# Gram-Schmidt beside an attention kernel: vectors kept as rows, the step's row spread by DMA

## What is computed

```python
def gram_schmidt(X):            # X: 256 x 32
    r = X.shape[1]
    Q = X
    for i in range(r):
        q = Q[:, i]
        q = q / (jnp.linalg.norm(q) + EPS)
        Q = Q.at[:, i].set(q)
        coeffs = q @ Q[:, i + 1:]
        Q = Q.at[:, i + 1:].add(-jnp.outer(q, coeffs))
    return Q
U_o = gram_schmidt(U)
V_o = gram_schmidt(V)
basis = U_o @ V_o.T
```

## Time and profile before

| | |
|---|---|
| runs | 1352.56, 1354.65, 1354.92 us |
| the profiled execution | 1352.78 us, of which 1350.6 us are the span of the trace |
| busy, share of the span | PE 96%, DVE 79%, ACT 80%, POOL 65% |
| mean granted TensorE clock | 0.988 of full speed |
| DMA | 175 MB, mean 130 GB/s |

### The profile page before, as it was taken

The page is one execution under the profiler, slowest core; times in us unless marked ns, Lnnn a source line. Parts: engine busy times, 40 slices in busy tenths (PEclk is TensorE's granted clock), DMA queues, the critical chain, the costliest instruction groups (busy, mean ns, idle before and its releaser), DMA issues. The chain is left out here.

```text
span 1350.6 us, 39501 instructions
## 1 busy us (share of the span) xinstructions
PE 1302.0 (96%) x11802; PEld 1101.9 (82%) x11802; DVE 1071.7 (79%) x3669; ACT 1084.2 (80%) x2697; POOL 871.8 (65%) x874
## 2 busy tenths in 40 slices
PE   4999999999999999999999999879999999999997
PEld 3777777777777777777777777559999999999996
DVE  4777787877778787777878778668888888888885
ACT  1788888888888888888888887867888888888873
POOL 4999989998998999899999989322222222222210
PEclk9999999999999999999999999979999999999998
DMA  9646555564655556465555674010101111111100
GB/s 288 191 146 211 174 183 181 173 210 146 211 169 186 178 175 205 150 211 166 190 174 179 203 224 133 25 32 25 47 31 47 31 46 31 39 38 34 43 25 32
DMA packets 182669, 175.05 MB, mean 130 GB/s; under 512 B 15552, under 2 KB 182112, under 8 KB 182624
## 3 DMA queue, kind: packets, MB, share of 16 engines
q1 hardware_dynamic: 181248, 173.64, 40.4%
q10 hardware_dynamic: 1376, 0.85, 0.2%
HBM read 157.69 MB, written 16.78 MB: 129 GB/s over the span
## 5 line engine op out<-in xcount | busy, mean ns | idle before, releaser
L430 POOL TENSOR_TENSOR ring<-ring,maskv 128x1024 f32<-128x1024 f32 x256 | 600.0, 2371 | 12.2 <-DMA ring<-in_fside 4.9
L917 ACT ACTIVATE ring<-ring,nmax 128x256 f32<-128x256 f32 x1024 | 452.6, 502 | 24.1 <-DVE nmax L601 24.1
L601 DVE CUSTOM_DVE_ANT_0 ring<-bank,ring 128x256 f32<-128x256 f32 x1024 | 373.1, 419 | 90.5 <-PE bank L1185 72.9
L922 ACT ACTIVATE pT<-bank 128x512 f32<-128x512 f32 x416 | 239.3, 592 | 102.0 <-PE bank L1200 101.9
L1200 PE MATMUL bank<-ident,ring 128*128 128x128 f32 x2048 | 292.3, 278 | 1.4 <-ACT pT L922 1.1
L1200 PEld LDWEIGHTS bank<-ident,ring 128*128 128x128 f32 x2048 | 231.7, 142 | 70.8 <-issue 47.9
L1052 ACT ACTIVATE work<-bank,b1t 128x256 f32<-128x256 f32 x256 | 107.6, 476 | 76.0 <-PE bank L1394 76.0
L1185 PE MATMUL bank<-work 32*128 32x256 f32 x2048 | 148.5, 404 | 6.0 <-DVE nmax L601 5.2
L1394 PE MATMUL bank<-hT_high,w_high 128*128 128x256 f32 x512 | 148.0, 289 | 4.3 <-DVE hT_rest L774 2.4
L1407 PE MATMUL bank<-w_high,gT_high 128*128 128x256 f32 x512 | 148.0, 289 | 0.0
L1394 PE MATMUL bank<-hT_rest,w_high 128*128 128x256 f32 x512 | 145.5, 284 | 0.0
(11 more groups left out here) (161 smaller groups left out, 2666.8 us busy)
## 6 DMA issues: line engine op xcount, KB each, us to landing
ring<-in_fside SPq DMA_DIRECT2D x128, 1024.0 KB, 7.6
xt<-in_x SPq DMA_DIRECT2D x32, 256.0 KB, 3.1
x_d<-x2s SPq DMA_DIRECT2D x32, 256.0 KB, 7.9
work<-x_d SPq DMA_DIRECT2D x32, 256.0 KB, 2.7
out<-pT SPq DMA_DIRECT2D x32, 256.0 KB, 2.2
mk<-in_mask SPq DMA_DIRECT2D x32, 64.0 KB, 6.7
w<-in_W SPq DMA_DIRECT2D x2, 1024.0 KB, 10.5
wada<-in_W_ada SPq DMA_DIRECT2D x1, 512.0 KB, 8.1
```

Of the source, the lines that this page charges most:

```text
L430: nc.gpsimd.tensor_tensor(v, v, m, ALU.add).then_inc(s_masked, 1)
L601: nc.vector.tensor_tensor_reduce(out=v, in0=score_ps[h % HG][:, qt], in1=v, scale=-1.0, scalar=ROW_MAX_NEG, op0=ALU.add, op1=ALU.min, accu ...
L917: nc.scalar.activation(v, v, ACT.Exp, bias=nmax[:, b.par, h, qt:qt + 1], scale=-1.0).then_inc(s_exp, 1)
L922: nc.scalar.activation(pT[:, h % (2 * HG)], tp_ps[h % 2], ACT.Copy).then_inc(s_pta, 1)
```

## The change

U and V are kept transposed, as 64 rows of 256 elements on 64 partitions (`uvT`, rows 0 to 31 for U and 32 to 63 for V). In batch i, SP writes all of `uvT` to a scratch tensor in memory (64 KB), waits until this has landed, and reads row i of U 32 times over into partitions 0 to 31 of `row` and row i of V into partitions 32 to 63 (two DMAs of 32 KB). DVE takes the products and the square as two multiplications with accumulation; POOL takes the root as before and a copy of `uvT` with row i cleared (`uvz`); DVE forms the coefficient and updates all rows in one operation. `gs_gram` on PE, all Gram-Schmidt work on ACT and POOL's `gs_update` are gone. At the start PE transposes U and V once, and at the end of stage 1 transposes them back (a new step of `response_matrix`).

```diff
+            def vector_rows(b):
+                sp.wait_ge(s_gupd, b.n + 1)
+                sp.dma_start(uv_d, uvT[:]).then_inc(s_uvst, 16)
+                sp.wait_ge(s_uvst, 16 * b.n + 16)
+                for a in range(2):
+                    sp.dma_start(row[a * R:(a + 1) * R], uv_d[bass.ds(b.n + a * R, 1)].rearrange("o d -> (o d)").partition_broadcast(R)).then_inc(s_row, 16)
...
             def gs_norm(i):
...
-                nc.gpsimd.tensor_tensor(nrm[:], gii[:], expo[:, 1], ALU.pow).then_inc(s_gp, 1)
+                nc.gpsimd.tensor_tensor(nrm[:], gii[:], expo[0:2 * R, 1, 0:1], ALU.pow).then_inc(s_gp, 1)
+                nc.gpsimd.tensor_scalar(uvz[:], uvT[:], keep[:, 0:1], 1.0, ALU.mult, ALU.mult).then_inc(s_gz, 1)
...
-                        ins = nc.gpsimd.tensor_scalar(gprod[:, a, c], coef[:, a], qcol[:, a, c:c + 1], 1.0, ALU.mult, ALU.mult)
-                nc.gpsimd.tensor_tensor(uv[:], uv[:], gprod[:], ALU.add).then_inc(s_gupd, 1)
...
             def gs_products(b):
-                dve.wait_ge(s_gram, i + 1)
-                nc.vector.tensor_copy(gii[:], gs_ps[:, :, bass.ds(i, 1)].rearrange("p a r -> p (a r)"))
-                nc.vector.scalar_tensor_tensor(gsb[:], gs_ps, -1.0, ahead, ALU.mult, ALU.mult).then_inc(s_gii, 1)
+                dve.wait_ge(s_row, 32 * b.n + 32)
+                nc.vector.tensor_tensor(keep[:], other[:, bass.ds(b.n, 1)], other[:, bass.ds(b.n, 1)], ALU.mult)
+                nc.vector.scalar_tensor_tensor(prods[:, 0], uvT[:], 1.0, row[:], ALU.mult, ALU.mult, accum_out=dot[:])
+                nc.vector.scalar_tensor_tensor(prods[:, 1], row[:], 1.0, row[:], ALU.mult, ALU.mult, accum_out=gii[:]).then_inc(s_gii, 1)
...
             def gs_reciprocal(i):
+                nc.vector.tensor_tensor(dotm[:], dot[:], ahead[:, bass.ds(i, 1)], ALU.mult)
                 nc.vector.reciprocal(rnrm[:], nrme[:]).then_inc(s_grec, 1)
+            def gs_share(i):
+                nc.vector.scalar_tensor_tensor(share[:], dotm[:], rnrm[:], own[:, bass.ds(i, 1)], ALU.mult, ALU.add).then_inc(s_gshare, 1)
+            def gs_coefficient(i):
+                nc.vector.tensor_tensor(coef[:], share[:], rnrm[:], ALU.mult).then_inc(s_gcoef, 1)
+            def gs_update(i):
+                dve.wait_ge(s_gz, i + 1)
+                nc.vector.scalar_tensor_tensor(uvT[:], row[:], coef[:], uvz[:], ALU.mult, ALU.add).then_inc(s_gupd, 1)
...
                     gs_reciprocal(b.plus(-1).n)
-                    reduces(b, (5, 6, 7))
+                    reduce_head(b, 5)
+                    gs_share(b.plus(-1).n)
+                    reduce_head(b, 6)
+                    gs_coefficient(b.plus(-1).n)
+                    reduce_head(b, 7)
+                    gs_update(b.plus(-1).n)
                     copy_pT(b, 3)
...
-                    gs_gram(b, n)
-                    gs_coefficients(b.plus(-1).n)
```

More of the change, by code:

```diff
@@ L132, in attention_block_kernel @@
         bvb = sb("bvb", [P, D]); bob = sb("bob", [P, D]); b2b = sb("b2b", [P, D]); cb = sb("cb", [P, D]); cb2 = sb("cb2", [P, D])
-        ident = sb("ident", [P, P]); later = sb("later", [P, R, R]); expo = sb("expo", [P, 2, 2])
+        ident = sb("ident", [P, P]); tri = sb("tri", [2 * R, 2 * R]); ahead = sb("ahead", [2 * R, R]); own = sb("own", [2 * R, R]); other = sb("other", [2 * R, R]); expo = sb("expo", [P, 2, 2])
         frq = sb("frq", [P, 1]); tti = sb("tti", [P, B], I32); ttf = sb("ttf", [P, B]); ang = sb("ang", [P, B])
@@ L139, in attention_block_kernel @@
         gw1 = sb("gw1", [P, DC, GW]); gb1 = sb("gb1", [P, GW]); gw2 = sb("gw2", [P, GW]); gb2 = sb("gb2", [P, 1]); gb2h = sb("gb2h", [P, 1])
-        uv = sb("uv", [P, 2, DC, R]); ucol = sb("ucol", [P, 2, DC]); gsb = sb("gsb", [P, 2, R]); gii = sb("gii", [P, 2])
-        nrm = sb("nrm", [P, 2]); nrme = sb("nrme", [P, 2]); rnrm = sb("rnrm", [P, 2]); qcol = sb("qcol", [P, 2, DC]); gprod = sb("gprod", [P, 2, DC, R]); coef = sb("coef", [P, 2, R])
+        uv = sb("uv", [P, DC, 2, R]); uvT = sb("uvT", [2 * R, D]); uvz = sb("uvz", [2 * R, D]); row = sb("row", [2 * R, D]); prods = sb("prods", [2 * R, 2, D])
+        dot = sb("dot", [2 * R, 1]); keep = sb("keep", [2 * R, 1]); gii = sb("gii", [2 * R, 1]); nrm = sb("nrm", [2 * R, 1]); nrme = sb("nrme", [2 * R, 1])
+        rnrm = sb("rnrm", [2 * R, 1]); dotm = sb("dotm", [2 * R, 1]); share = sb("share", [2 * R, 1]); coef = sb("coef", [2 * R, 1])
         respT = sb("respT", [R, D]); gram = sb("gram", [R, HG, R]); t1 = sb("t1", [R, D])
@@ L361, in _ @@
             nc.gpsimd.memset(ident[:], 0.0)
-            nc.gpsimd.memset(later[:], 1.0)
+            nc.gpsimd.memset(tri[:], -1.0)
             nc.gpsimd.memset(expo[:, 0], -0.5)
@@ L367, in _ @@
                                     pattern=[[-1, P]], channel_multiplier=1)
-            nc.gpsimd.affine_select(out=later[:], in_=later[:], compare_op=ALU.is_gt, fill=0.0, base=0,
-                                    pattern=[[-1, R], [1, R]], channel_multiplier=0).then_inc(s_const, 1)
+            nc.gpsimd.affine_select(out=tri[:], in_=tri[:], compare_op=ALU.is_gt, fill=0.0, base=0,
+                                    pattern=[[-1, 2 * R]], channel_multiplier=1).then_inc(s_const, 1)
             pool.wait_ge(s_const, 1)
@@ L532, in _ @@
             ins.then_inc(s_perm, 1)
+            for a in range(2):
+                rows = slice(a * R, (a + 1) * R)
+                nc.vector.tensor_copy(ahead[rows], tri[rows, a * R:(a + 1) * R])
+                nc.vector.tensor_copy(own[rows], ident[rows, a * R:(a + 1) * R])
+                link(nc.vector.tensor_scalar(other[rows], ident[rows, a * R:(a + 1) * R], -1.0, 1.0, ALU.mult, ALU.add))
             nc.vector.memset(half[:, 0:1], 0.0)
@@ L577, in gs_products @@
[L577 to L579 removed]
+                    dve.wait_ge(s_gnrm, b.n)
+                nc.vector.tensor_tensor(keep[:], other[:, bass.ds(b.n, 1)], other[:, bass.ds(b.n, 1)], ALU.mult)
+                nc.vector.scalar_tensor_tensor(prods[:, 0], uvT[:], 1.0, row[:], ALU.mult, ALU.mult, accum_out=dot[:])
@@ L932, in ctxT_out @@
                 nc.scalar.activation(ctxT[:], tail_ps, ACT.Copy).then_inc(s_ctxT, 1)
[L934 to L952, removed]
             def yn_out(b):
@@ L1007, in body @@
                 if main:
-                    gs_column(b.n)
                     copy_pT(b, 8)
@@ L1209, in pv @@
                         pe.wait_ge(s_ctxn, 2 * b.n)
+                    else:
+                        pe.wait_ge(s_gupd, 1)
                 if g == 1:
@@ L1297, in _ @@
             pe.wait_ge(s_load_att, 16 * len(loads_att))
+            vectors_transposed()
             project_v(first)
-            x_back(first, False)
+            x_back(first)
             def y_transpose(b):
@@ L1369, in body @@
                 if prep:
-                    x_back(b.plus(1), True)
+                    x_back(b.plus(1))
                 if main:
```

85 lines of the change are left out of this document (44 added, 41 removed).

## The result

The changed kernel takes 1696.34 us (median of four runs, 1691.09 to 1698.91), the kernel before 1354.2 beside it: the ratio is 1.252, interval 1.250 to 1.254. The profiled execution took 1693.84 us, of which 1692.0 are the span of the trace. The increase is 342 us where 394 were forecast; the time lies inside the range.

What follows compares the result with a forecast made beforehand. PE's own order was taken to set 26.29 us a batch. Terms summed to 39.15, 12.86 more, over 30 batches: 1352.8 + 386 + 8 - 1 = 1746 profiled, 1748 us as median; range 1585 to 1815.

Steps and rivals of the forecast that it cites:

- T to R: From transposes 7 done and SP issuing the first bias half (T) to the row's landing (R): 11.8 us a batch.
- R to transposes 13: From the row's landing through DVE's products, statistics and copy 11 to PE's transposes 13: 2.3 us.
- first clock loss: After PE's 6.7 us idle for the row, the clock is at half for 3.5 us: 1.75 us lost (0.9 to 2.6).
- stall at copy 3: PE waits at transposes 5 for DVE's delayed copy 3: 4.0 us taken, 4.4 worked out, 3.2 if share slips ahead.
- second clock loss: Slow PE clock behind the stall at copy 3: 1.3 us a batch, bounds 0 and 1.75.
- The queue: The row's store waits behind 2 MB of bias in SP's queue, landing at 476.9; the row is there at 479.5.
- Small operations against POOL: DVE's dotm, share, coef and update, with both operands in SBUF, wait for POOL's additions; bounds 0.14 and 2.35 us each.
- batch 30: Row in time, but DVE's products meet POOL (two waits, 4.3 us) and later operations wait (4): +8 us.
- without a clock loss: Rival: both waits come but the clock holds, 36.1 us a batch, about 1655 us; chance 0.05.
- PE's own order sets the period.: Stage 1 before the change: PE's order sets 26.29 us a batch; the other engines have slack.
- faster: Rival: PE's freed 0.81 us is kept if the row lands early and small operations pass POOL: 1340 us; chance 0.04.
- Costs put at nothing: ACT's and POOL's removed operations and the transposes at start and end: 0, the transposes with 2 us either way.

Runs made afterwards that it cites:

- the row put first: Changed kernel with the row's store and two loads ahead of the first bias half in SP's order: 1570.2 us, ratio 1.159.
- the one-operand version: Changed kernel with keep, dotm, share and coef written with one tensor operand, the other a per-partition scalar (keep: constant 1.0): 1576.0 us, ratio 1.164.
- the one re-ordering of PE that was tried there: Kernel without any step in the loop, with project_o between transposes 12 and 13: 1334.17 us, ratio 0.985.
- two moves more: Row first and one-operand small operations, plus project_o between transposes 12 and 13 (1347.52 us), then also the update ahead of copy 7 (1337.56 us).
- the two edits: Changed kernel with the row first in SP's order and the small operations with one tensor operand: 1356.7 us together, ratio 1.0019.
- the run without the step: Changed kernel with the whole Gram-Schmidt step left out of the loop: 1336.77 us, ratio 0.987.
- the later update: DVE's update moved from ahead of copy 3 to ahead of copy 7, tried only on top of the other three edits: 1337.56 us, ratio 0.9896.
- project_o's move: project_o of the batch before put between transposes 12 and 13, on top of row first and one-operand small operations: 1347.52 us, ratio 0.9956.

## Why the prediction was right, and where its sum was off

| term, us a batch | predicted | the batch shown | mean of the 29 long periods |
|---|---|---|---|
| T to R | 11.8 | 517.19 - 505.87 = 11.32 | 11.03 |
| R to transposes 13 | 2.3 | 519.42 - 517.19 = 2.23 | 2.22 |
| from there until PE wants transposes 5, with the first clock loss | 11.35 + 1.75 = 13.1 | 535.50 - 2.82 - 519.42 = 13.26 | 13.48 |
| stall at copy 3 | 4.0 | 2.82 | 3.18 |
| to the next T, with the second clock loss | 6.65 + 1.3 = 7.95 | 543.91 - 535.50 = 8.41 | 7.99 |
| period | 39.15 | 38.04 | 37.90, by R 37.96 |

(The 18.0 us of the prediction stand here as 11.35 and 6.65.)

- **The queue.** Right, and shown by the row put first: DVE's wait goes. The size was 0.8 us too long in the mean. The rows are issued at T + 8.7 (514.58 - 505.87) where I had the store landing at T + 9.2, and a load lands in 1.8 us, near the lower bound that I had named (1.7), and not in 2.1.
- **The wait reaches PE at copy 11.** Right: transposes 13 start 2.2 us behind R.
- **Small operations against POOL.** Right, and shown by the one-operand version: the same arithmetic takes 0.20 us. The measurement also agrees with what the SBUF — State Buffer page of the Trainium skill says in "SBUF: two separate sides" of a DVE instruction with two SBUF inputs beside a GpSimd instruction that reads SBUF, down to 64 x 1 elements.
- **The stall at copy 3.** This is the other term that was mis-sized, 4.0 for 3.18 in the mean. In the batch shown DVE came to dotm where I had it (R + 11.7 for 11.8), and PE wanted transposes 5 where I had them (R + 15.5 for 15.4). There are two long waits, as forecast. But I let share meet the first addition, 0.9 us after dotm; it came in front of it, coef met that addition and the update the next. So the second wait falls on the last of the four, nothing of the step is left behind it, and copy 3 starts at R + 17.5 where I had 19.2. The prediction had named this case (3.2) and taken a value nearer to the other. It is the case of 17 of the 29 batches; in 9 of the other 12 copy 3 does start at R + 19.1, and PE, itself later there, waits 3.2 to 3.5 us. That all four operations can wait isn't that all four do: what decides is how they fall on the 0.8 us between POOL's additions, and little turns it: share passed where it came at R + 12.50 (the batch shown) and waited 2.2 us where it came at R + 12.66 (the batch whose row is there at 933.27).
- **The clock.** Both sizes were near: half until about 522.9, the second loss 8.41 - 6.65 = 1.76 in the batch shown and 7.99 - 6.65 = 1.34 in the mean, for 1.3. What was wrong is what hangs on the first. It is a term of PE's own way to transposes 5, and what keeping the clock gives there is taken back by the stall and the clock behind it: the time is the same. So the bounds of 0.9 and 2.6 us for it were bounds of nothing, and the rival "without a clock loss" (1655) took 1.75 us off that aren't to be had as long as POOL's sequence ends later. All bounds taken together also give 1648 to 1838 us, wider than the 1680 to 1815 of the sum's own range.
- **How often.** 29 periods were long, not 30, at 37.96 us: 29 x 11.67 = 338. The next took 1193.28 - 1160.38 = 32.9 us and the last 25.8; with some -3 at the ends that is the 341 of the profiled execution. Of the 52 us too much, 29 x (39.15 - 37.96) = 35 lie in the period, 6 in the thirtieth, and the rest mainly in batch 30, whose +8 for products that meet POOL didn't come: POOL was waiting in front of its root, as in the other batches.

- **"PE's own order sets the period."** Half right. The freed 0.81 us is worth 0.48 with everything else gone, and the one re-ordering of PE that was tried there gave nothing clear on top. The rival "faster" (1340) named a place that exists: 1337.56 was reached with its two conditions met, the row early and the small operations past POOL, and with two moves more that it hadn't named. With its conditions alone the time is that of the kernel before.
- **Costs put at nothing.** ACT's and POOL's relief and the transposes at both ends moved nothing that could be seen; by the table, what is unexplained at the ends is about -3 us.

Why are the two edits together worth 94 us more than their sum? The same 24 periods (from the products of the fourth batch to those of the 28th) in the kernel after, with the row first, with one operand, and with both:

```profile
172.99:1084.27 911.28, 702.37 (x5856) 523.12 (x5856) 607.11 (x2256) 520.28 (x1200) 548.51 (x432) 0.90 0.41 130
160.55:968.62 808.07, 688.00 (x5857) 512.57 (x5856) 639.16 (x2257) 521.71 (x1201) 549.69 (x432) 0.90 0.46 146
160.82:980.48 819.66, 672.20 (x5856) 502.13 (x5856) 543.31 (x2257) 518.60 (x1200) 552.62 (x432) 0.91 0.45 144
137.76:773.73 635.97, 624.89 (x5858) 467.11 (x5856) 526.07 (x2259) 516.39 (x1201) 554.85 (x432) 1.00 0.58 186
```

The span less PE's busy time is its idle time: 8.7, 5.0, 6.1 and 0.5 us a period. The busy time of the same products is 29.3, 28.7, 28.0 and 26.0 us, and what is over 26.0 is the slow clock. So the small operations left alone cost 7.2 us a period and the late row left alone 7.7, together 14.8, and both at once only 11.5: whichever edit comes first gives back no more than 4.3 of these. Of the 3.35 us between, 2.0 are idle time and 1.4 clock. Most of the idle part is one place: with the row first PE waits 4.53 us at transposes 5, with both causes 3.2, since it gets there late itself. 3.35 us times 29 are 97 us, the 94 of the measurement.

What stays open: half of the 0.33 us a batch that the run without the step doesn't give back, and how much the later update would give without project_o's move.

## What to carry to other kernels

Two stalls in one period are not two terms of a sum: work out for each meeting point the time of every chain that leads there, take the latest, and charge a slow clock only on the chain that is the latest. A tiny transfer that a serial step waits for goes in front of the bulk loads of its queue, and a tiny DVE operation beside a busy POOL takes its second factor as a scalar per partition. Repair both before judging a design by either, since one of them alone showed little over a third of what the pair gave.

## What was new on the hardware

- A 64 x 1 DVE product with two SBUF tensors takes 0.14 us alone and up to 2.37 beside a POOL addition; with the factor as a scalar per partition 0.20, at most 0.21 in 32 batches, also beside an addition.
- A store of 64 KB to memory lands after 7.5 us behind 2 MB on its queue and after 1.9 in front of them; a load of 32 KB that spreads one row over 32 partitions lands after 1.8.
- 44 transposes of 0.11 us each in a gap of 5 to 6 us kept the granted clock at the upper level behind it: the eight output products took 1.89 us in place of 3.12 to 3.16. It was worth nothing in the kernel after and 2.25 us a batch in the one-operand version.
